# Sparse attention on one core: two rounds of weighting back to back, and the score products reordered between them

## What is computed

```python
xn = _layernorm(x)
x = x + attn(xn, q_w, k_w, v_w, o_w, o_b, unity_scale) + ffn(xn, weight_fp8, bias, ...)
# attn: key j is allowed for query i where (j % 4 == 0) | (abs(i - j) <= 8)
q = q * sigmoid(unity_scale)
scores = einsum('bhqd,bhkd->bhqk', q, k) / sqrt(16)
scores = where(allowed, scores, -inf)
out = einsum('bhqk,bhkd->bhqd', softmax(scores), v) @ o_w + o_b
```

## Time and profile before

| | |
|---|---|
| time, median of three runs | 1394.42 us (1392.87 to 1395.8) |
| the profiled execution: time, span | 1392.68 us, 1390.9 us |
| TensorE busy | 1301.3 us, 94% |
| VectorE, ScalarE, GpSimd busy | 1077.6, 841.3, 265.2 us |
| mean granted TensorE clock | 0.965 of full speed |
| a step in the steady state | 15.28 us |

### The profile page before, as it was taken

One profiled execution on the slowest core, in us unless ns is written; L12 is line 12 of the kernel. 1 busy time (PEld: TensorE's weight loads), 2 busy tenths in 40 slices (PEclk: granted clock), 3 DMA queues, 4 the chain that ended last, 5 costly groups with the idle time before them and its releaser, 6 DMA issues.

```text
span 1390.9 us, 29034 instructions
## 1 busy us (share of the span) xinstructions
PE 1301.3 (94%) x9792; PEld 640.5 (46%) x9792; DVE 1077.6 (77%) x2583; ACT 841.3 (60%) x1524; POOL 265.2 (19%) x382
## 2 busy tenths in 40 slices
PE   6698888879999999999999999999999999999996
PEld 4466666633444444434444443444344344444385
DVE  7999999868888787878777887878787778888232
ACT  2333333415777777767777776777677667777800
POOL 5444444330011111111111111111111111111100
PEclk9799999977999999999999999999999999999998
DMA  5566666972353544435353544445353525442258
GB/s 184 149 188 194 188 187 183 208 205 43 90 106 104 111 105 104 114 90 120 101 109 92 122 105 99 101 106 116 94 112 99 110 87 121 105 105 92 73 188 287
DMA packets 207843, 177.28 MB, mean 127 GB/s; under 512 B 48784, under 2 KB 184592, under 8 KB 206160
## 3 DMA queue, kind: packets, MB, share of 16 engines
q1 hardware_dynamic: 201168, 168.20, 47.4%
q10 hardware_dynamic: 6528, 7.08, 1.6%
HBM read 106.14 MB, written 68.29 MB: 125 GB/s over the span
## 4 chain that ended last, share of the span: by engine, by line
PE 74%; issue 1%; DVE 1%; DMA 1%; ACT 1%; ACTq 0%; POOL 0%; DVEq 0%; POOLq 0%
PE ps_attend L925 18%; PE ps_attend L886 18%; PE ps_attend L910 18%; PE ps_attend L932 5%; PE ps_attend L894 4%; PE ps_attend L891 4%; PE ps_attend L911 4%; PE ps_attend L1018 3%; DVE masked L857 1%; DMA q_op<-attn_dram 1%; PE ps_attend L883 1%; ACT probs L806 0%; ACT probs L811 0%; ACT out_rows L785 0%; DVE base L866 0%
## 5 line engine op out<-in xcount | busy, mean ns | idle before, releaser
L857 DVE CUSTOM_DVE_ANT_0 masked<-ps_attend,max_mask 128x620 bf16<-128x620 f32 x1024 | 783.5, 798 | 213.5 <-PE ps_attend L911 201.2
L806 ACT ACTIVATE probs<-ps_attend 128x512 f32<-128x512 f32 x1024 | 569.2, 596 | 205.9 <-PE ps_attend L886 195.3
L910 PE MATMUL ps_attend<-k_op,q_op 96*128 96x512 bf16 x1024 | 395.7, 393 | 10.6 <-POOL k_op L672 7.1
L886 PE MATMUL ps_attend<-q_op,k_op 99*128 99x512 bf16 x1024 | 374.2, 388 | 15.0 <-issue 14.7
L925 PE MATMUL ps_attend<-probs,v_op 128*32 128x512 f32 x2048 | 275.7, 611 | 0.1
L911 PE MATMUL ps_attend<-k_op,q_op 96*128 96x108 bf16 x1024 | 218.4, 213 | 0.0
L886 PEld LDWEIGHTS ps_attend<-q_op,k_op 99*128 99x128 bf16 x1024 | 91.1, 97 | 244.4 <-ACT probs L806 153.1
L690 POOL CAST negmax<-peak 128x16 bf16<-128x16 f32 x64 | 12.6, 196 | 854.9 <-DVE peak L857 854.9
L910 PEld LDWEIGHTS ps_attend<-k_op,q_op 96*128 96x128 bf16 x1024 | 100.0, 98 | 135.6 <-DVE peak L857 67.7
L811 ACT ACTIVATE probs<-ps_attend 108x512 f32<-108x512 f32 x256 | 152.7, 598 | 12.3 <-PE ps_attend L894 1.7
L911 PEld LDWEIGHTS ps_attend<-k_op,q_op 96*128 96x128 bf16 x1024 | 102.3, 100 | 52.1 <-issue 1.4
(11 more groups left out here) (70 smaller groups left out, 1066.8 us busy)
## 6 DMA issues: line engine op xcount, KB each, us to landing
k_op<-k_parts_dram SPq DMA_DIRECT2D x96, 256.0 KB, 4.9
q_op<-q_parts_dram SPq DMA_DIRECT2D x384, 64.0 KB, 2.7
v_dram<-v_sb SPq DMA_DIRECT2D x64, 256.0 KB, 3.3
share_rows<-shares_dram SPq DMA_DIRECT2D x64, 256.0 KB
attn_dram<-out_rows SPq DMA_DIRECT2D x64, 256.0 KB, 4.2
v_op<-v_dram SPq DMA_DIRECT2D x48, 288.0 KB
q_parts_dram<-qk_parts SPq DMA_DIRECT2D x48, 256.0 KB, 4.1
k_parts_dram<-qk_parts SPq DMA_DIRECT2D x48, 192.0 KB, 2.2
```

The costliest lines, as they stand in the source:

```text
L806: ins = nc.scalar.activation(probs[:, r, h], ps_s[st.bank(kind)], ACT.Exp)
L857: nc.vector.tensor_tensor_reduce(masked[:, i % 2], ps_u[i % 2][:, 0:UNIT], keep["max_mask"][:, mask], 1.0, -3e38, ALU.add, ALU.max, peak[: ...
L886: ins = nc.tensor.matmul(bank, k[0:KM, h * S + r * P:h * S + (r + 1) * P], q[:, h], start=True, stop=True)
L910: nc.tensor.matmul(ps_u[i % 2][:, 0:NS], cols, k[0:KR, h * S:h * S + NS], start=True, stop=True)
```

## The change

Nothing is added or removed. TensorE's order changes, and with it `SCORES` (ScalarE's order) and the places of `copy_out` and `move_negmax` on ScalarE:

```diff
 SCORES = (
-    ("far", 0, 0), ("far", 0, 1), ("far", 0, 2), ("negmax",), ("far", 0, 3),
-    ("far", 1, 0), ("far", 1, 1), ("far", 1, 2), ("near", 0), ("far", 1, 3),
-    ("near", 1), ("near", 2), ("far", 2, 0), ("far", 2, 1), ("far", 2, 2),
-    ("far", 2, 3), ("far", 3, 0), ("far", 3, 1), ("far", 3, 2), ("near", 3),
+    ("far", 0, 0), ("far", 0, 1), ("far", 0, 2), ("far", 0, 3), ("far", 1, 0),
+    ("negmax",), ("far", 1, 1), ("near", 0), ("near", 1), ("far", 1, 2),
+    ("far", 1, 3), ("near", 2), ("far", 2, 0), ("far", 2, 1), ("far", 2, 2),
+    ("far", 2, 3), ("near", 3), ("far", 3, 0), ("far", 3, 1), ("far", 3, 2),
     ("far", 3, 3),
 )
...
-                    if kind == ("far", 1, 1) and st.n >= 1:
+                    if kind == ("far", 1, 3) and st.n >= 1:
                         copy_out(st)
                     if ("negmax",) in todo:
-                        if kind == ("far", 0, 3) or st.n == -1:
+                        if kind == ("far", 1, 1) or st.n == -1:
                             move_negmax(st)
```

More of the change, by code:

```diff
@@ L961, in weigh_own @@
                         weigh(st, 0, r)
+                ahead(0)
                 far(0, 0)
-                ahead(0)
+                far(0, 1)
                 ahead(1)
-                far(0, 1)
                 far(0, 2)
-                weigh_last(3)
+                far(0, 3)
                 ahead(2)
-                maxima()
-                far(0, 3)
                 far(1, 0)
                 ahead(3)
+                weigh_last(3)
+                weigh_last(4)
+                ahead(4)
+                maxima()
+                ahead(5)
                 far(1, 1)
-                ahead(4)
-                weigh_last(4)
-                ahead(5)
+                near(0)
+                ahead(6)
+                near(1)
+                ahead(7)
                 far(1, 2)
-                ahead(6)
-                near(0)
                 far(1, 3)
-                ahead(7)
-                near(1)
                 ahead(8)
                 near(2)
+                ahead(9)
                 far(2, 0)
-                ahead(9)
                 far(2, 1)
@@ L990, in body @@
                 weigh_own(0)
+                weigh_own(1)
                 far(2, 2)
@@ L994, in body @@
                 ahead(12)
+                near(3)
                 far(3, 0)
-                weigh_own(1)
+                ahead(13)
                 far(3, 1)
-                ahead(13)
+                ahead(14)
                 far(3, 2)
-                near(3)
-                ahead(14)
                 far(3, 3)
```

## The result

The changed kernel takes 1450.81 us, the median of four runs (1449.43 to 1453.55), against 1393.99 for the kernel before (1392.87 to 1395.8): a ratio of 1.0409, with a 95% interval of 1.0389 to 1.0429. It is slower, as forecast, but by 56.8 us where the forecast had 12.6. Its profiled execution took 1453.55 us, with a span of 1451.7, which is 60.8 over the span before (1390.9).

The account below looks back on a forecast made before the run. The prediction took TensorE's own order as the bound. Steps 4.4, the end 0.6 and late keys 8.6 gave 13.6 us on 1392.7, so 1406.3, taken as 1407.0 against the median; range 1396 to 1416.

Parts of the forecast that it names:

- The merges: On TensorE, two places per step where weightings stand together save 0.21 us each, 0.41 per step, 26 us in all.
- the rule on weight loads: Rival: TensorE can't load a second weighting's weights ahead, each merge gives only 0.09 us; +15, so 1422; chance 0.05.
- The new waits: TensorE waits for score banks and unit buffers, 0.49 us per step against 0.41 saved; step 15.36, 4.4 us in all.
- The keys: Keys issued behind the later copy-out make u0 wait 0.95 us at nine changes of iteration, 8.6 us in all.
- The sums: Sums' load on SP's queue, issued at 11.97, lands 5.5 later at 17.5, before VectorE's reciprocal needs it: hidden, no cost.
- share_rows: Issued on SP's queue at 11.3, lands at 17.6; GpSimd's product and the out_rows store come later, but hidden.
- The clock: Rival: new 1 us waits lower TensorE's clock more often, each drop 1.7 us; ten of them 1424; chance 0.06.
- The sum: Whole kernel: 4.4 for steps, 0.6 for the end, 8.6 for keys, 13.6 us; 1406.3 from the profiled execution, taken as 1407.0.
- its own correction for the median: The profiled execution, 1392.7 us, lies 1.7 below the median of the runs, with which the sum is to be compared.

Follow-up runs that it names:

- e1: The changed kernel, with SP issuing the second piece of keys or values ahead of its wait for the copy-out; 1398.9 us.
- e6: The changed kernel, with the second piece of keys issued ahead of the copy-out wait in the first step of an iteration only; 1414.3 us.
- e3: The kernel before, with only the copy-out moved 2.7 us later on ScalarE, behind near(1); 1446.7 us.
- e11: The changed kernel, with the sums' store, its landing and the sums' load put ahead of the second piece of keys and share_rows; 1486.7 us.
- e2: The changed kernel, with VectorE's reciprocal of the sums ahead of its ninth maximum of a step instead of its fifth; 1434.8 us.
- e10: The kernel before, with the copy-out 2.7 us later and the second piece of keys or values issued ahead of the copy-out wait; 1392.4 us.
- e8: Against the kernel before: another TensorE order merging only W0 and W1, copy-out behind near(0), maxima's DMA with far(2,0), second piece issued first; 1384.9 us.
- e5: The changed kernel, with the copy-out two entries earlier on ScalarE, behind far(1,1) instead of far(1,3); 1405.6 us.

## Why the prediction was wrong, and what of it held

**The merges: right.** Both kinds of pair stand 0.88 apart, and the exit takes 1.00 (after, to compare with the earlier trace rows):

```profile
703.97 1.92 PE L925 MATMUL ps_attend<-probs,v_op 128*32 128x512 f32 x16
705.83 0.39 PE L886 MATMUL ps_attend<-q_op,k_op 99*128 99x512 bf16 x1
...
712.64 1.06 PE L925 MATMUL ps_attend<-probs,v_op 128*32 128x512 f32 x8
713.52 1.06 PE L932 MATMUL ps_attend<-probs,v_op 108*32 108x128 f32 x32
714.51 0.39 PE L910 MATMUL ps_attend<-k_op,q_op 96*128 96x512 bf16 x1
```

705.83 - 703.97 = 1.86 for two rounds of L925, 0.88 + 0.98; L932 follows L925 after 0.88. By the rule on weight loads that the prediction weighed (the Trainium skill, TensorE: Matmul & The Clock Gate, section Part 3, The mechanism) each would have taken 1.00; it does not hold for these loads.

**The new waits: right, to 0.06.** The steps were to be 15.36 and are 15.30 to 15.34. That f03, f13, u14 wait as worked out shows in where they stand: f03 at 1.34 from the step's start, u14 at 13.21 to 13.25, W2 at 14.31 to 14.34 (worked out: 1.35, 13.24, 14.32). e1, the new order without the late loads, came out 4.1 us over the kernel before of the same rounds (1394.7), where the sum had 5.0; that close it is by luck, since its steps are a little shorter than worked out, and 1.7 us of it are clock ((23.9 - 20.5) / 2).

**The keys: right in mechanism, but not what decided.** e6 shows the waits of 0.95 as 0.7 on average. In the changed kernel another stall ahead of them hid all but one, or two: a wait of 1.06 at 1293.7, listed as issue, also ends 0.09 us behind the landing of the last keys.

**The sums: this step failed.** "The sums would be issued at 11.97 and land 5.5 later, at 17.5, [...] hidden." Its 5.5 is the median of all 64 loads. The one that is issued in the first step of an iteration, behind two k loads and share_rows, took 4.7 to 8.1 even in the kernel before, 7.0 in the median of that place; the single DMA above shows 7.4. With that the working would have read 11.97 + 7.4 = 19.4, against a maximum of u4 that starts no sooner than 15.36 + 4.8 = 20.2: 0.8 us to spare instead of the 2.7 that looked safe. The trace of before says the same without any working: in its first steps the sums were there 2.8 to 4.2 us ahead of the reciprocal, and the copy-out was to move by 3.06.

The time to landing also did not stay as it was when the issue moved. It grew to 9.2 to 12.6, and VectorE waited 1.8 to 4.9 us. In the kernel before, SP issues the next q loads 5.5 us behind the sums' load; now they come 3.0 behind it (805.47 to 808.45), into the same traffic. Shown by e1, e3 and e11: the copy-out's time and the large loads ahead make the difference. The Trainium skill, DMA: Bandwidth & Descriptors, section Queues, rings and completion order, says that each DMA engine consumes one queue's descriptors in ring order; e11 agrees (1.6 us with nothing large ahead), and by it alone the q loads behind would matter little. The two k loads ahead and the six q loads behind, in the step shown above:

```profile
L75 SPq DMA_DIRECT2D k_op<-k_parts_dram x2: 422/432/441, 803.9 to 804.4; - x2
...
DMA to landing us min/median/max: 5.3/6.2/7.0
```
```profile
L82 SPq DMA_DIRECT2D q_op<-q_parts_dram x6: 592/594/608, 808.5 to 811.7; - x6
...
DMA to landing us min/median/max: 3.1/3.7/8.6
```

The k loads are in by 811.4, 6.6 us before the sums (2.8 in the same place before). Four of the six q loads, issued behind the sums' load, land before it, at 811.6 to 814.3. So the last 6 us of the 12.6 were spent beside share_rows and the q loads, with the k loads gone. Yet in e1, where the k loads went out some 6 to 8 us ahead of the sums', the q loads follow it by 0.9 to 2.2 us in the first steps, and it lands in 2.4 to 2.9. The q loads alone don't do it; how much of the growth is theirs once the k loads have held things up, and how much share_rows', no run here shows apart.

**share_rows: hidden, as argued, in time but not in waits.** SP's wait L749 for GpSimd's product rose from 5.2 us (3 times) to 84.2 (29 times). It stands ahead of the wait for the copy-out, which comes later, and TensorE sees none of it. e11 shows what it costs where the copy-out is not the later one.

**The clock: right in kind, mis-sized.** The prediction gave 0.06 to drops behind 1 us waits, at 1.7 each. Waits of that size made hardly any: none behind e6's waits for the keys, none behind the stalls of 0.4 to 0.9 in the changed kernel, one behind its two of 1.5. Its six stalls of 2.5 to 3.5 us were each followed by half clock. These seven stretches are 41.0 us of the 75.1; the other 34.1 stand behind the six ways back, 13.7 more than before. The clock was priced as its own rival, when it belonged to any stall as a second charge.

**The sum.** The terms of the prediction add up to 13.6 us, or 1408.0 by its own correction for the median; it took 1407.0 and gives no reason. That changes nothing here.

**The 60.8 us together**, spans of the two profiled executions:

| | us |
|---|---|
| units waiting for VectorE, that is for the sums | 25.8 |
| half clock behind these stalls: 41.0 / 2 | 20.5 |
| more half clock behind the ways back: (34.1 - 20.5) / 2 | 6.8 |
| loop's way back, longer pauses: 17.3 - 14.7 | 2.6 |
| keys, once in the list and once as issue | 2.1 |
| steps 0.02 longer, every fourth 0.06: 62 x 0.03 | 1.9 |
| attention starts later (first maxima 313.4 against 310.8) | 2.6 |
| sum | 62.3 |

That is 1.5 too much. The half clock's terms are bounds, since TensorE is not busy through all of it (6.56 of 6.80 us above). The 2.6 at the start may be plain scatter of the two executions, which isn't shown. The size of the pauses at the way back (2.4 to 3.3 in most kernels, up to 4.2 in e3 and 4.6 in e2) is unexplained too.

## What to carry to other kernels

Whoever moves an instruction moves all that stands behind it in every in-order queue that waits for it; work out for each of these when it lands against when it is needed, and take the landing from the DMAs at that very place, not from the median of their line. Issue ahead of a wait what does not need the wait: the second piece moved up was worth 52 us of the 57, and e1 and e10 differ from the two slow kernels in nothing else. Price a stall of two to three us twice, once for itself and once for the half clock that followed most of them here.

## What the runs showed of the hardware

- One 8 KB load on SP's queue lands in 1.6 us (median) with nothing large ahead of it (e11), in 2.6 with share_rows issued 2.9 us ahead of it (e1), in 4.7 to 8.1 behind two 256 KB k loads and share_rows (before), and in 9.2 to 12.6 in the same company some 3 us later (after; 9.4 to 12.3 in e3).
- DMAs of one queue don't land in the order of their issue: four q loads issued 3.0 to 4.9 us behind the sums' load landed 3.7 to 6.5 us before it (after, at 811.6 to 814.3 against 818.0).
- Stalls of TensorE of 2.5 to 3.5 us were mostly followed by 3.4 or 6.8 us at a granted clock of 0.50 (1.2 GHz), the longer one shown above; e2 has two of 1.8 and 2.1 with 3.4 behind, and e11's stalls of up to 6.8 had up to 10.2. How long it lasts varied and isn't explained.
- The way back of TensorE's loop costs a pause of 2.4 to 3.0 us each time in the kernels before and e8, and the clock behind it: 31.8 us over six ways back.
- Weight loads of fp32 weightings that all take the same 128 rows overlap the matmuls before them: 0.88 apart, against 1.00 with bf16 work behind.
- A DMA issue on ScalarE's queue holds the activation behind it for 0.83 us where it stands alone (after: issue 700.44, next activation 701.27, with nothing else to wait for), and for nothing more where it is issued along with an activation that runs anyway (e5). In the earlier trace rows the activation at 782.07 also waited for its matmul.
